# Two layers of cross attention and mixture of experts on one core: expert sums, root guesses and late steps of the second attention in another order

## The reference

```
x = x + L0_xattn(layernorm(x), ctx, ctx, ...)   # 16 heads of width 16, rotary, softmax, output projection
x = x + L0_ffn(layernorm(x), ...)               # 16 experts, top 2 by a grouped router, relu^2, shared part
x = x + L1_xattn(layernorm(x), ctx, Wq, Wk, Wv) # 32 heads of width 8, RMS norm on q and k, softmax
x = x + L1_ffn(layernorm(x), ...)               # base W, plus 16 low-rank experts of rank 16, top 2 by logits
```

## Time and profile before

| | |
|---|---|
| median of 3 runs | 370.22 us (368.12, 371.21, 370.22) |
| the profiled execution | 370.5 us, of which the span from first to last instruction 368.8 us |
| mean granted TensorE clock | 0.912 |
| TensorE busy | 294.5 us, 80% |
| VectorE busy | 264.8 us, 72% |
| ScalarE busy | 185.2 us, 50% |
| GpSimd busy | 113.3 us, 31% |
| the loop of stage C | first exponential at 261.2 us, last at 335.3 us |

### The profile page before, as it was taken

One profiled execution on the slowest core, in us unless ns is written; L12 is line 12 of the kernel. 1 busy time (PEld: TensorE's weight loads), 2 busy tenths in 40 slices (PEclk: granted clock), 3 DMA queues, 4 the chain that ended last, 5 costly groups with the idle time before them and its releaser, 6 DMA issues.

```text
span 368.8 us, 7376 instructions
## 1 busy us (share of the span) xinstructions
PE 294.5 (80%) x2676; PEld 182.9 (50%) x2676; DVE 264.8 (72%) x675; ACT 185.2 (50%) x334; POOL 113.3 (31%) x224
## 2 busy tenths in 40 slices
PE   4337878888887776899995998966878888969796
PEld 3212344344343332487684986853544555544364
DVE  6967889889898896678943454527478888678872
ACT  1111465665756657625441677623557778743211
POOL 1134364463543222161771112057400000202300
PEclk9955799999999999969997899995599999987899
DMA  7594269478684202300226366946445766300002
GB/s 242 168 270 115 88 173 285 134 219 262 170 261 132 73 23 74 111 2 1 101 100 188 125 230 230 331 136 192 130 138 164 228 181 175 102 2 1 0 30 85
DMA packets 68435, 52.29 MB, mean 142 GB/s; under 512 B 4784, under 2 KB 65200, under 8 KB 68400
## 3 DMA queue, kind: packets, MB, share of 16 engines
q1 hardware_dynamic: 62768, 40.84, 36.8%
q10 hardware_dynamic: 4096, 6.79, 5.8%
q0 software_dynamic: 1536, 4.20, 3.6%
HBM read 30.38 MB, written 21.23 MB: 140 GB/s over the span
## 4 chain that ended last, share of the span: by engine, by line
PE 42%; DVE 29%; POOL 8%; issue 8%; DMA 6%; ACT 5%; SPq 2%; DVEq 0%; POOLq 0%
DVE mx L1749 10%; PE psum L1112 5%; PE psum L747 4%; POOL sorted_x L1647 4%; PE psum L997 4%; PE psum L1125 4%; PE psum L783 4%; POOL low L1651 3%; PE psum L732 3%; PE psum L1088 3%; PE psum L768 2%; PE psum L874 2%; ACT prob L1251 2%; PE psum L1215 2%; DVE rope_ab L1738 2%
## 5 line engine op out<-in xcount | busy, mean ns | idle before, releaser
L1749 DVE TENSOR_REDUCE mx<-psum 128x2 f32<-128x512 f32 x128 | 81.1, 684 | 16.0 <-PE psum L747 15.4
L1251 ACT ACTIVATE prob<-psum 128x1024 f32<-128x1024 f32 x64 | 64.5, 1023 | 37.6 <-PE psum L768 37.3
L747 PE MATMUL psum<-kstk,qstk 64*128 64x256 bf16 x256 | 27.4, 296 | 26.3 <-DVE mx L1749 15.0
L783 PE MATMUL psum<-prob,vt 128*32 128x256 f32 x512 | 34.3, 385 | 6.2 <-ACT prob L1251 5.1
L1474 ACT ACTIVATE prob<-psum 128x1024 f32<-128x1024 f32 x32 | 32.5, 1023 | 0.2 <-PE psum L1072 0.2
L747 PEld LDWEIGHTS psum<-kstk,qstk 64*128 64x128 bf16 x256 | 8.7, 97 | 43.1 <-DVE mx L1749 28.7
L542 POOL TENSOR_TENSOR parts<-qk_rest,parts 128x256 bf16<-128x256 f32 (+1 forms) x15 | 13.8, 920 | 51.3 <-ACT parts L1411 47.7
L1088 PE MATMUL psum<-prob,vt 128*32 128x128 f32 x512 | 21.9, 292 | 5.4 <-ACT prob L1474 5.3
L768 PE MATMUL psum<-qstk,kstk 64*128 64x256 bf16 x256 | 24.9, 279 | 0.8 <-DMA qstk<-mT 0.8
L783 PEld LDWEIGHTS psum<-prob,vt 128*32 128x32 f32 x512 | 13.9, 109 | 18.5 <-ACT prob L1251 7.4
L1258 ACT CAST parts<-qk 128x512 bf16<-128x512 f32 x8 | 4.9, 618 | 31.4 <-POOL qk L536 16.8
(11 more groups left out here) (281 smaller groups left out, 624.6 us busy)
## 6 DMA issues: line engine op xcount, KB each, us to landing
qstk<-stack_scratch SPq DMA_DIRECT2D x30, 256.0 KB, 3.8
stack_scratch<-parts SPq DMA_DIRECT2D x22, 192.0 KB, 2.1
kstk<-key_scratch SPq DMA_DIRECT2D x16, 256.0 KB, 3.8
kstk<-stack_scratch SPq DMA_DIRECT2D x14, 256.0 KB, 5.8
stack_scratch<-parts SPq DMA_DIRECT2D x24, 128.0 KB, 2.1
low<-in_wup ACTq DMA_DIRECT2D x4, 640.0 KB, 4.5
wdn<-in_wdn ACTq DMA_DIRECT2D x4, 640.0 KB, 5.8
prob<-sorted_x SPq DMA_DIRECT2D x8, 256.0 KB, 4.2
```

The costliest lines, as they stand in the source:

```text
L747: last = nc.tensor.matmul(banks[s][:, nb * D:(nb + 1) * D], qstk[par][rows, pair, nb * P:(nb + 1) * P], kstk[par][rows, pair, :], start=Tr ...
L783: last = nc.tensor.matmul(pv_bank(1)[32 * j:32 * j + 32, g * D:(g + 1) * D], vt[b % 2][:, mb, 4 * t + j, 8:40] if low else vt[b % 2][:, mb ...
L1251: nc.scalar.activation(prob[(b * PAIRS + k) % 3][:], exp_buf(k).rearrange("p a n -> p (a n)"), ACT.Exp, scale=SCALE).then_inc(exp_done, 1)
L1749: nc.vector.tensor_reduce(mx[:, half, :, 4 * s + p4:4 * s + p4 + 1], bank.rearrange("n (b m) -> n b m", b=2), AX_X, ALU.max).then_inc(misc ...
```

## The change

It moves instructions, and adds one wait on GpSimd. Nothing that is computed changes.

1. The expert sums of block b + 4 stand at spot 4 of block b, after the addition of `o(b - 1)`, for b = 0 to 3. The later `attend_norm` is called with `added=True`. The statistics and centering of block 3 stand ahead of the loop.
2. `guess_roots(b + 2)` stands behind the second exponential of blocks 1 to 5; in block 0 that of `q(2)` stands behind the fourth.
3. The first bfloat16 part of `qT(2)` is made behind the first exponential of block 1 and not behind the last of block 0.
4. `v(1)` moves from spot 0 to spot 4 of block 0.
5. In block 7 `wide(1)` and `dlg(0)` (with `picks(0)`) change places; ScalarE takes `wide(1)` out behind the second exponential, and `gap_exp(0)` stands in the last step.
6. On TensorE `wide(4)` follows `wide(3)`, ahead of `dxT(6)`.
7. VectorE: `ln_stats(4, 2)` ahead of `silu(0)`; `weights_of(0)` between `silu(1)` and `silu(2)`.
8. GpSimd waits for the third SiLU before it adds the bias to block 4 and those behind it.

```diff
         D_EARLY = {(5, 7): [("dxT", 0), ("dxT", 1)], (6, 1): [("dxT", 2), ("dxT", 3)], (6, 3): [("wide", 0)],
-                   (6, 5): [("dh", 0)], (7, 1): [("dlg", 0)], (7, 3): [("wide", 1)], (7, 5): [("dxT", 4), ("dxT", 5)],
+                   (6, 5): [("dh", 0)], (7, 1): [("wide", 1)], (7, 3): [("dlg", 0)], (7, 5): [("dxT", 4), ("dxT", 5)],
...
-            u = [("v", b + 1)] if spot == 0 and b + 1 < NB else []
+            u = [("v", b + 1)] if spot == 0 and 0 < b < NB - 1 else []
             if b == 0:
-                u += {1: [("xT", 2)], 3: [("q", 2)], 6: [("qT", 2)]}.get(spot, [])
+                u += {1: [("xT", 2)], 3: [("q", 2)], 4: [("v", 1)], 6: [("qT", 2)]}.get(spot, [])
...
             wide(3)
+            wide(4)
             ring("dxT", 6)
             ring("dh", 1)
             ring("dxT", 7)
             ring("dh", 2)
-            wide(4)
             ring("dlg", 1)
...
                     if k == 0:
                         if b == 1:
+                            first_parts_c(full("qT", 2), bank_of("qT", 2), 0, 0)
                             second_parts_c(gone_v("qT", 2), 0)
                         if 0 < b < NB - 2:
                             squares(b + 2, full("q", b + 2), bank_of("q", b + 2))
-                            guess_roots(b + 2)
...
                     if k == 1:
+                        if 0 < b < NB - 2:
+                            guess_roots(b + 2)
...
+                        if b == 7:
+                            take_wide(1)
...
                     if k == 2:
                         if b == 0:
                             squares(2, full("q", 2), bank_of("q", 2))
-                            guess_roots(2)
...
-                        if b >= 6:
-                            take_wide(b - 6)
-                        if b == 7:
-                            gap_exp(0)
+                        if b == 6:
+                            take_wide(0)
                     if k == 3:
                         if b == 0:
-                            first_parts_c(full("qT", 2), bank_of("qT", 2), 0, 0)
+                            guess_roots(2)
...
                             take_dxT(5)
+                            gap_exp(0)
                             take_wide(2)
...
             for b in range(NB):
                 pool.wait_ge(xn_ready, 3 * NB + b + 1)
+                if b == 4:
+                    pool.wait_ge(silu_done, 3)
...
                 elif kind == "q":
                     sum_squares(b)
-                    if b < 7:
-                        attend_norm(b + 1, 1)
+                    if 2 < b < 7:
+                        attend_norm(b + 1, 1, added=True)
                         center(b + 1, (b + 1) % 2)
-                    else:
+                    elif b == 7:
...
             center(2, 0)
+            attend_norm(3, 1)
+            center(3, 1)
...
+                    if spot == 4 and b + 4 < NB:
+                        add_experts(b + 4, 1)
                     if b == 5 and spot == 4:
                         ln_normalize(2)
                         ln_normalize(3)
-                    if b == 7 and spot == 4:
-                        weights_of(0)
                     if b == 6 and spot == 4:
-                        silu(0)
                         dve.wait_ge(misc_free, gone_v("o", 5))
                         ln_stats(4, 2)
+                        silu(0)
...
             silu(1)
+            weights_of(0)
             silu(2)
```

## The result

The changed kernel takes 372.46 us (median of 20 runs, 369.81 to 375.37) against 369.83 for the kernel before beside it (20 runs): ratio 1.006, 95% interval 1.0033 to 1.0087, so 1.2 to 3.2 us slower, about 2.2. The forecast was 369.8 us and a gain of 0.7. The profiled execution took 372.66 us (span 370.9) against 370.5 (span 368.8).

The account below looks back on a forecast made before the run. It took the order of waits to bind: an 8.29 us circle between VectorE and TensorE, no engine full. Terms -3.3 (blocks 0 to 4), -0.6 (blocks 6 and 7) and +3.2 (tail) gave -0.7: 369.8 us from 370.5, range 365.5 to 372.5.

Parts of the forecast that it names:

- the queries' round trip: Second attention's loop: query reads through DRAM allow a 7.41 us period; 0.3 us of waiting in the first one.
- blocks 6 and 7: Statistics ahead of `silu(0)`, `wide(1)` in a gap, picks later: -0.6 us up to `wide(3)`, bounds -2.5 and 0.
- the price of the low clock in the tail: `dlg(1)` to `flip_wxa(2)`: 5 us of low TensorE clock behind a 4 us pause, +2.3 us, bounds 0 and 3.4.
- Expert sums and roots: Loop period 8.29 to 7.41 us: sums save 1.03, late roots lose 0.15; 3.5 us over four periods.
- The second rival: Loop: the queries' round trip holds the cycle at 8.1 us, total 372.2 us; chance 0.12 together with late roots.
- Block 0: Block 3's statistics ahead of the loop, second division at 273.4 for 273.54: -0.1 us, bounds 0 and the 2.39 wait.
- The tail: From `wide(3)` on: `dlg(1)` 0.9 us later plus 2.3 us of low TensorE clock behind a pause, +3.2 us.
- The step of 0.9: Tail: `silu(1)` at W + 5.2, then weights and `silu(2)`, put `dlg(1)` at W + 10.4, 0.9 us later.
- GpSimd's bias rows: Four additions of 0.7 us beside the second half's picks: counted 0, with 0.5 us kept for the range.
- The first (full clock): Clock stays full through both pauses or rises at once: gain 4.9, total 365.6 us; chance 0.25.
- The third: Loop: roots behind the second exponential come too late, -0.5 for the blocks, 372.5 us; chance 0.12 together with the second.
- The fourth: Tail: four POOL additions in series with the picks, +1.7 us, total 371.5 us; chance 0.06.

Follow-up runs that it names:

- early half: Kernel before with only the loop's parts (expert sums, roots, block 3 ahead of the loop, block 0's casts and `v(1)`): 366.5 us, ratio 0.9938.
- late half: Kernel before with only the changes to block 7, `wide(4)`, VectorE's order in the tail and GpSimd's wait: 374.54 us, ratio 1.0132.
- pause filled: Changed kernel computing `wide(4)` three times, the last two between `dh(2)` and `dlg(1)`: 368.84 us, ratio 0.9967 to the kernel before.
- pause shortened: Changed kernel with `wide(4)` back ahead of `dlg(1)` and `weights_of(0)` moved behind `ln_stats(6, 1)`: 368.19 us, ratio 0.994 to the kernel before.
- two versions of the bank order: Changed kernel with `o(6)` ahead of `dlg(0)`, wide products and `weights_of(0)` moved; second also drops GpSimd's wait: ratios 0.9856 and 0.9888 to before.
- the first experiment: Changed kernel with `wide(4)` moved back between `dh(2)` and `dlg(1)`: 370.93 us, ratio 1.0032 to the kernel before.

## Why the prediction was wrong, by its steps

The mechanism was seen, and the sign of the whole was not: of two large terms of opposite sign, the gain came out 0.6 us smaller (2.7 for 3.3) and the cost 1.4 us larger (4.0 for 2.6). Three steps failed: the queries' round trip (1.7 us of waits for 0.3), blocks 6 and 7 (+0.5 for -0.6) and the price of the low clock in the tail (+3.1 for +2.3).

*Expert sums and roots.* Right in the main, with two small terms that made up for each other. The undisturbed period is 7.38 us (7.41 forecast). The 0.15 us for late roots did not come: the guess ends at 292.71, `rs` starts without a wait at 292.75, and `qkn` stands 3.69 us behind pvT, for 4.70 before. Instead the sums cost 0.1 us in their new place, which I had called covered: beside GpSimd's third part they take 1.29 us, not 0.99, fill all of the 1.13 us of idle time, and pvT follows `qkn` by 3.69 us instead of 3.59. Block 4, without sums at spot 4, has 7.24 to 7.27.

*The queries' round trip, +0.3.* This step failed. It measured 1.7 us here and 1.95 in the early half alone. I took 7.19 us between two reads before as proof that such a cycle is to be had. But it was the shortest of four intervals (7.45, 7.19, 8.40 and 8.12), and short because its first read came late (the write ahead of it landed in 2.8 us) and its second early (1.6); the writes themselves were 8.45 us apart. So it said nothing of a cycle of 7.2, and in the faster loop the last write takes 2.7 to 3.6 us. Why it does is open. The second rival named this place and priced it too high: the periods are 7.8 on the mean, not 8.1.

*Block 0, -0.1.* Its size is not settled. In this pair 13.75 became 13.03 us, -0.7, between the bounds given (0 and the 2.39 us wait for `xn`). But the late half alone, whose block 0 is that of the kernel before, has 13.06, and the profiles with the new block 0 have 12.66 to 13.81. Taken with the four periods behind it the gain stands clear: from the first scores to pvT of `divide_c(4, 1)` it is 46.98 and 47.07 us with the old loop, 44.29 in the changed kernel and 44.43 in the early half. `v(1)`, which I had put at nothing, took TensorE 2.08 us ahead of the first products with V; with it moved the first pvT stands 5.75 us behind the first scores, for 7.16 (6.76 in the late half). The second division does not keep that.

*Blocks 6 and 7, -0.6.* This step failed, and the result, +0.5, lies above its upper bound of 0. The picks started 25.01 us behind pvT of block 4, not 24.2 (24.01 before). The missing 0.8 us stands in two rows: `rs_a` took 0.43 for 0.12 and `rstd` 0.65 for 0.16, since `take_wide(1)`, moved forward, let GpSimd's two additions run just there. The late half alone shows the same two rows (0.42 and 0.65). The rest is as worked out: 3.64 us from the picks' start to `dxT(5)` (3.6 forecast), then the low level all the way, 5.43 us to `wide(3)` for 5.7. I had given the full level a share of 0.6 for which the trace held no reason. So 0.8 of the 1.1 us between forecast and result is a collision of VectorE with GpSimd that has no term in the sum, and the rest is this share, less 0.3.

*The tail, +3.2.* Right in mechanism and nearly in size (+3.5): `dlg(1)` 9.90 us behind `wide(3)` (10.4 forecast), a pause of 3.91 us (4), the low clock behind it. The term of 2.3 was too small: the clock was low for 6.3 us, not for the 5 that I took as a mean of 6.8 and 3.25. The 3.25 us of `wide(4)` was a stretch that was low for the most part (granted clock 0.50 from 345.90 to 349.30), not one behind a pause of 4 us. The step of 0.9 was too large by 0.5: `silu(1)` starts at W + 4.87, not 5.2, and it and the weights take 1.71 and 1.38 us, not 1.86 and 1.48. That it is the pause ahead of `dlg(1)` that brings the clock down is shown by two runs that end it in different ways, filled or shortened: 7.44 and 7.45 us for 10.06.

*GpSimd's bias rows, 0.* The four additions cost VectorE 1.1 us: `weigh` 1.28 for 0.75, the picks 3.79 for 3.24. They are covered by TensorE at its low clock (it runs without a gap from 351.57 to 358.89), as the prediction has it. At full clock they are not quite: `dlg(1)` to `flip_wxa(2)` is 7.44 and 7.45 us with them (pause filled, pause shortened), 6.95 and 7.02 without (kernel before, early half); in the two versions of the bank order it is 7.44 and 6.81. `hot_t` at 351.15 took 0.77 us for 0.22 and ended at 351.92, where the last addition ends at 351.83. The Trainium skill (SBUF — State Buffer, "SBUF: two separate sides") says that a VectorE instruction with two SBUF inputs and a GpSimd instruction that reads SBUF shut each other out, for the whole instruction of the one that started first. The trace agrees: `hot_t`, which reads `sel_s` and `top`, ended when the addition had, while the two instructions ahead of it, with one SBUF input each, took 0.23 and 0.22 us beside the same additions, which kept 0.75 each.

*The rivals.* The first (full clock) fell in the change as made; in the tail it is the kernel with the pause filled. The second named 372.2 us, next to what was measured, but not by its terms: it has 0.9 us of gain in blocks 0 to 4 and 2.6 of cost, and 2.7 and 4.0 were measured. The third fell: from block 1 on nothing waits for the roots. The fourth's collision is there, 1.1 us of it, but behind the low clock, where it adds nothing.

*The drift of 0.8 us* ahead of the second attention belongs to no step.

## What to carry to other kernels

Before a filler is taken out of the gap in front of an engine's late stretch, or VectorE's work is put ahead of what TensorE waits for, price the pause with the clock that may fall behind it: here pauses of 2.00 and 3.91 us in the tail each cost 2.6 us more behind them. A cycle through DRAM has to be tested against the faster loop with the slowest landing seen, not with the shortest interval seen. And a change of independent halves should be timed in halves: this one was 2.3 us of gain and 4.9 of loss.

## What the runs showed of the hardware

- TensorE's clock stayed at 1.00 behind a pause of 2.39 us and one of 0.61, and was 0.52 behind one of 2.00 us in the first experiment. In the old tail, behind pauses of 1.30 to 1.55, 0.27 and 0.55 us, `wide(4)` took 1.98 and 1.99 us in two profiles and 3.16 to 3.41 in three. The pause's length alone does not decide it.
- Eight redundant matmuls in a pause shortened the kernel by 3.4 us (ratios 1.006 and 0.9967).
- A 64 KB write to DRAM on SyncE's queue landed in 1.6 to 3.3 us in the loop as before and in 1.6 to 4.5 in the faster one and its variants.
- VectorE instructions of 0.12 to 0.22 us took 0.43 to 0.77 beside GpSimd's additions; the additions took 0.73 to 0.75 each, 0.70 in a row of three before.
